# Attention with routed experts: the work behind PV two steps earlier, and the last unit of four pairs split into three and one

## The reference, cut to what matters

```python
x = x + xattn(layernorm(x), ctx_1024, ctx_1024, mask)      # softmax(q k^T / sqrt(8)) v, then Wo
...
xt = layernorm(x)
router_probs = softmax(xt @ Wr + br)
gates = max(router_probs);  idx = argmax(router_probs)
xn = layernorm(xt) * ln_g + ln_b
h = relu(xn @ W1[idx] + b1[idx])
y = (h @ W2[idx] + b2[idx]) * gates
return x + y
```

## Time and profile before

| | us |
|---|---|
| median of 3 runs (lowest to highest) | 333.48 (331.01 to 342.68) |
| the profiled execution | 330.89 |
| its span, first to last instruction | 329.2 |
| busy: PE, DVE, ACT, POOL | 253.6, 222.8, 175.0, 141.0 |

### The profile page before, as it was taken

The page is one execution under the profiler, slowest core; times in us unless marked ns, Lnnn a source line. Parts: engine busy times, 40 slices in busy tenths (PEclk is TensorE's granted clock), DMA queues, the critical chain, the costliest instruction groups (busy, mean ns, idle before and its releaser), DMA issues.

```text
span 329.2 us, 8922 instructions
## 1 busy us (share of the span) xinstructions
PE 253.6 (77%) x3112; PEld 200.9 (61%) x3112; DVE 222.8 (68%) x674; ACT 175.0 (53%) x342; POOL 141.0 (43%) x158
## 2 busy tenths in 40 slices
PE   2488999989887879888779576008897989899980
PEld 0335766767565657565667575007786878788880
DVE  6427977887788787677765545723776768677770
ACT  1528786766746584757315311006665756676640
POOL 3812343245473773634713407730443334344442
PEclk9999999999999999999965855556999999999996
DMA  8999999999999700000000001011111211212100
GB/s 233 288 252 212 279 249 206 283 271 288 257 281 291 180 19 11 27 10 2 27 8 10 28 0 34 33 42 44 41 47 45 63 50 43 60 55 65 46 28 0
DMA packets 49611, 36.31 MB, mean 110 GB/s; under 512 B 3087, under 2 KB 45460, under 8 KB 49568
## 3 DMA queue, kind: packets, MB, share of 16 engines
q1 hardware_dynamic: 46864, 31.11, 41.1%
q0 software_dynamic: 2272, 4.27, 4.0%
q10 hardware_dynamic: 432, 0.38, 0.5%
HBM read 14.11 MB, written 22.09 MB: 110 GB/s over the span
## 4 chain that ended last, share of the span: by engine, by line
issue 42%; SPq 30%; DVE 14%; DMA 6%; DVEq 3%; PE 2%; POOL 1%; POOLq 1%
SPq L240 16%; SPq L276 8%; DVE hT L701 4%; DMA out<-ot,G 4%; DVE xh L689 3%; DVE ot L710 3%; SPq L246 2%; DMA G<-rows_dram 2%; DVE yb L708 2%; DVEq L678 2%; SPq L249 2%; SPq L252 1%; PE ps L838 1%; DVE WR L681 1%; DVE VB L483 1%
## 5 line engine op out<-in xcount | busy, mean ns | idle before, releaser
L415 ACT ACTIVATE PT<-ps 128x512 f32<-128x512 f32 x64 | 35.4, 595 | 62.0 <-PE ps L757 59.6
L388 POOL DMA_INDIRECT out<-ot,G x39 | 39.8, 1020 | 65.9 <-DVE ot L710 64.9
L549 DVE TENSOR_REDUCE mx<-ps 128x16 f32<-128x1024 f32 x32 | 39.2, 1225 | 36.5 <-PE ps L733 36.4
L746 PEld LDWEIGHTS ps<-VB,PT 128*64 128x64 f32 x1024 | 35.8, 148 | 17.3 <-issue 17.3
L838 PE MATMUL ps<-xg,WR 128*128 128x128 f32 x312 | 45.3, 290 | 0.0
L746 PE MATMUL ps<-VB,PT 128*64 128x18 f32 x1024 | 38.8, 220 | 4.6 <-ACT OT L408 3.2
L849 PE MATMUL ps<-WR,hT 128*128 128x128 f32 x312 | 41.1, 275 | 0.0
L365 POOL TENSOR_TENSOR Kb<-KT,hmask 128x512 f32<-128x512 f32 x32 | 33.1, 1041 | 18.4 <-PE ps L733 18.1
L838 PEld LDWEIGHTS ps<-xg,WR 128*128 128x128 f32 x312 | 39.4, 198 | 1.4
L419 ACT ACTIVATE Pr<-Pr,rowany 128x1024 f32<-128x1024 f32 x32 | 36.7, 1148 | 5.8 <-DVE Pr L579 5.8
L579 DVE TENSOR_TENSOR Pr<-ps,mx 128x1024 f32<-128x1024 f32 x32 | 39.1, 1221 | 0.3
(11 more groups left out here) (121 smaller groups left out, 387.7 us busy)
## 6 DMA issues: line engine op xcount, KB each, us to landing
rows_dram<-empty SPq DMA_DIRECT2D x32, 528.0 KB, 9.7
WA<-in_wpk SPq DMA_DIRECT2D x8, 578.0 KB
G<-rows_dram SPq DMA_DIRECT2D x39, 66.0 KB, 1.8
X<-in_x SPq DMA_DIRECT2D x8, 256.0 KB, 7.0
C<-in_ctxT SPq DMA_DIRECT2D x8, 256.0 KB, 6.4
XT<-in_xT SPq DMA_DIRECT2D x8, 256.0 KB, 7.3
out<-ot,G POOLq DMA_INDIRECT x39, 2.3
rows_dram<-row,posi POOLq DMA_INDIRECT x32
```

The lines of the kernel that those rows point to most:

```text
L388: g.indirect_dma_start(out=out, out_offset=bass.IndirectOffsetOnAxis(ap=G[:, q, D + 1:D + 2].bitcast(I32), axis=0), in_=ot[:, q, :], in_of ...
L415: a.activation(PT[:, p % 2, 512 * m:512 * m + 512], ps[:, 4 + m, :], ACT.Copy).then_inc(freed[4 + m], 1)
L549: v.tensor_reduce(out=mx[:, i % 2, :], in_=psS.rearrange("p g (i k) -> p g i k", k=S), axis=AX.X, op=ALU.max).then_inc(s_mx, 1)
L746: last = mm(psPV[64 * b:64 * b + 64, 18 * j:18 * j + 18], PT[:, p % 2, 128 * j + 64 * b:128 * j + 64 * b + 64], VB[:, p // GP % 3, 2 * (p ...
```

## The change

Everything behind PV comes closer to it. The new stations, by lag: `onT` 2, at the end of TensorE's step instead of 3; copy to `OT` 3; `o0`, `o1` 3 and 4; `residual` 4 and 5; `ve2` 5; `pow` and `iota` 5, now at the end of GpSimd's step instead of the start; `lgm` to `lmx` 6; `lsub` to `oh` and `lex` 7; `seen` 8; `r` 9, and 8 for the last three units; `pt2` to the gate one step behind `r`; scatters 10 to 13. `xb` stays at lag 2. The last four pairs become a unit of three (28 to 30) and one of one pair (31), so there are nine units; a unit of three has all its output products in one piece. The scatters of the last three units are issued together, in one step at lag 9. Some small tiles get two buffers. The loop ends two steps earlier.

```diff
@@ -27,9 +27,10 @@
 WP = F + FC * D + FC + D
 GP = 4
 NG = NP // GP
-NU = NG
+UNITS = [(GP * g, GP) for g in range(NG - 1)] + [(NP - 4, 3), (NP - 1, 1)]
+NU = len(UNITS)
 UR = 4
-FIRST, LAST = -10, NP + 11
+FIRST, LAST = -10, NP + 9
 
 
 def wait(eng, sem, value):
@@ -40,8 +41,23 @@
 
 def unit_at(step, lag):
...
-    return u if rest == 0 and 0 <= u < NU else None
+    return next((u for u, (first, n) in enumerate(UNITS) if first + n - 1 + lag == step), None)
+
+
+def unit_of(p):
+
+    return next(u for u, (first, n) in enumerate(UNITS) if first <= p < first + n)
+
+
+def ranked_at(step):
+
+    return next((u for u, (first, n) in enumerate(UNITS) if first + n - 1 + (9 if u < NU - 3 else 8) == step), None)
+
+
+def part(u, m):
+
+    n = UNITS[u][1]
+    return range(0, min(n, 2) if n == GP else n) if m == 0 else range(2, n if n == GP else 2)
 
...
-        for name, lag in (("onT", 3), ("o0", 4), ("o1", 5), ("r", 10)):
-            if (u := unit_at(i, lag)) is not None:
+        for name, u in (("o0", unit_at(i, 3)), ("o1", unit_at(i, 4)), ("r", ranked_at(i)), ("onT", unit_at(i, 2))):
+            if u is not None and (name != "o1" or len(part(u, 1))):
                 bank[6].append((name, u))
...
-        psO = ps[:, 6, 0:2 * OW].rearrange("p (k c) -> p k c", c=OW)
+        psO = ps[:, 6, 0:3 * OW].rearrange("p (k c) -> p k c", c=OW)
...
-                if (u := unit_at(i, 7)) is not None:
-                    pool.wait_ge(s_ve2, 2 * u + 2)
-                    g.tensor_tensor(out=row[:, u % UR, :, OW + 3:RT], in0=ve2[:, u % 2, :, :],
-                                    in1=half[:, None, :].to_broadcast([P, GP, 2]), op=ALU.pow).then_inc(s_rs2, 1)
-                    g.iota(row[:, u % UR, :, OW + 1:OW + 2].bitcast(I32), pattern=[[P, GP], [0, 1]], base=GP * P * u,
-                           channel_multiplier=1).then_inc(s_tok, 1)
...
                 if (u := unit_at(i, 2)) is not None:
-                    pool.wait_ge(x_in[u], 16)
+                    first, n = UNITS[u]
+                    pool.wait_ge(x_in[first // GP], 16)
                     wait(pool, freed[6], nth("weights", 2) if u == 0 else 0)
                     if u >= 2:
-                        pool.wait_ge(freed[6], nth("o1", u - 2))
-                    g.tensor_tensor(out=xb[:, u % 2, :, E:OW], in0=X[:, GP * u:GP * u + GP, :],
-                                    in1=bo_e[:, None, E:OW].to_broadcast([P, GP, D]), op=ALU.add).then_inc(s_xb, 1)
-                for k in range(GP):
-                    if (u := unit_at(i, 11 if k == 0 or i + 1 == LAST else 11 + k)) is not None:
-                        if k == 0:
-                            pool.wait_ge(s_nm2, u + 1)
-                            pool.wait_ge(s_tok, u + 1)
-                            pool.wait_ge(s_gate, u + 1)
-                            pool.wait_ge(s_pos, u + 1)
+                        pool.wait_ge(freed[6], last_o(u - 2))
+                    g.tensor_tensor(out=xb[:, u % 2, 0:n, E:OW], in0=X[:, first:first + n, :],
+                                    in1=bo_e[:, None, E:OW].to_broadcast([P, n, D]), op=ALU.add).then_inc(s_xb, 1)
+                for u, (first, n) in enumerate(UNITS):
+                    late = u >= NU - 3
+                    at = i - (first + n - 1 + (9 if late else 10))
+                    if at == 0:
+                        pool.wait_ge(s_nm2, u + 1)
+                        pool.wait_ge(s_tok, u + 1)
+                        pool.wait_ge(s_gate, u + 1)
+                        pool.wait_ge(s_pos, u + 1)
+                    for k in range(n) if late and at == 0 else [at] if not late and 0 <= at < n else []:
                         scatter(u, k)
+                if (u := unit_at(i, 5)) is not None:
+                    first, n = UNITS[u]
+                    pool.wait_ge(s_ve2, 2 * u + 2)
+                    g.tensor_tensor(out=row[:, u % UR, 0:n, OW + 3:RT], in0=ve2[:, u % 2, 0:n, :],
+                                    in1=half[:, None, :].to_broadcast([P, n, 2]), op=ALU.pow).then_inc(s_rs2, 1)
+                    g.iota(row[:, u % UR, 0:n, OW + 1:OW + 2].bitcast(I32), pattern=[[P, n], [0, 1]], base=P * first,
+                           channel_multiplier=1).then_inc(s_tok, 1)
...
-                if (u := unit_at(i, 4)) is not None:
+                if (u := unit_at(i, 3)) is not None:
                     act.wait_ge(filled[6], nth("onT", u))
                     if u >= 1:
-                        act.wait_ge(filled[6], nth("o1", u - 1))
-                    a.activation(OT[:], ps[:, 6, :], ACT.Copy).then_inc(freed[6], 1)
+                        act.wait_ge(filled[6], last_o(u - 1))
+                    n = UNITS[u][1]
+                    a.activation(OT[:, 0:P * n], ps[:, 6, 0:P * n], ACT.Copy).then_inc(freed[6], 1)
                 if 0 <= i - 1 < NP:
...
-                if (u := unit_at(i, 9)) is not None:
+                if (u := unit_at(i, 7)) is not None:
...
+                if (u := unit_at(i, 4)) is not None:
+                    residual(u, 0)
                 if (u := unit_at(i, 5)) is not None:
-                    residual(u, 0)
-                if (u := unit_at(i, 6)) is not None:
                     residual(u, 1)
-                if (u := unit_at(i, 11)) is not None:
+                if (u := ranked_at(i - 1)) is not None:
+                    n = UNITS[u][1]
                     dve.wait_ge(filled[6], nth("r", u))
-                    v.tensor_tensor(out=pt2[:], in0=psR.rearrange("p (k e) -> p k e", e=E), in1=oh[:, u % 2, 1:GP + 1, :],
+                    v.tensor_tensor(out=pt2[:, u % 2, 0:n, :], in0=psR[:, 0:E * n].rearrange("p (k e) -> p k e", e=E), in1=oh[:, u % 2, 1:n + 1, :],
...
-                if (u := unit_at(i, 8)) is not None:
+                if (u := unit_at(i, 6)) is not None:
+                    n = UNITS[u][1]
                     dve.wait_ge(s_rs2, u + 1)
-                    v.tensor_tensor(out=lgm[:], in0=row[:, u % UR, :, 0:E], in1=row[:, u % UR, :, OW + 4:RT].to_broadcast([P, GP, E]),
+                    v.tensor_tensor(out=lgm[:, u % 2, 0:n, :], in0=row[:, u % UR, 0:n, 0:E], in1=row[:, u % UR, 0:n, OW + 4:RT].to_broadcast([P, n, E]),
                                     op=ALU.mult).then_inc(s_lgm, 1)
-                    v.scalar_tensor_tensor(out=row[:, u % UR, :, OW:OW + 1], in0=mv2[:, u % 2, :, 0:1], scalar=-1.0,
-                                           in1=row[:, u % UR, :, OW + 3:OW + 4], op0=ALU.mult, op1=ALU.mult).then_inc(s_nm2, 1)
...
-                if (u := unit_at(i, 3)) is not None:
-                    pe.wait_ge(freed[6], nth("onT", u) - 1)
-                    for k in range(GP):
-                        last = nc.tensor.transpose(ps[:, 6, P * k:P * k + P], On[:, (GP * u + k) % 8, :], ident[:])
-                    last.then_inc(filled[6], 1)
                 for m in range(2):
-                    if (u := unit_at(i, 4 + m)) is not None:
-                        pe.wait_ge(t_in[u], 16)
+                    if (u := unit_at(i, 3 + m)) is not None and len(part(u, m)):
+                        first = UNITS[u][0]
+                        pe.wait_ge(t_in[first // GP], 16)
                         pe.wait_ge(freed[6], nth(f"o{m}", u) - 1)
-                        for k in range(2):
-                            c = P * (2 * m + k)
-                            mm(psO[:, k, :], OT[:, c:c + P], Wox, start=True, stop=False, skip_group_check=True)
-                            last = mm(psO[:, k, 0:E], XT[:, GP * P * u + c:GP * P * u + c + P], Wrc[:],
+                        for k in part(u, m):
+                            o = psO[:, k - part(u, m)[0], :]
+                            mm(o, OT[:, P * k:P * k + P], Wox, start=True, stop=False, skip_group_check=True)
+                            last = mm(o[:, 0:E], XT[:, P * (first + k):P * (first + k + 1)], Wrc[:],
                                       start=False, stop=True, skip_group_check=True)
                         last.then_inc(filled[6], 1)
-                if (u := unit_at(i, 10)) is not None:
+                if (u := ranked_at(i)) is not None:
+                    n = UNITS[u][1]
                     wait(pe, s_const, 17 if u == 0 else 0)
                     pe.wait_ge(s_oh, u + 1)
                     wait(pe, s_seen, u)
                     pe.wait_ge(freed[6], nth("r", u) - 1)
-                    for k in range(GP):
-                        mm(psR[:, E * k:].rearrange("p (k e) -> p k e", e=E), ones[:],
-                           oh[:, u % 2, k:k + 1, :].to_broadcast([P, GP - k, E]), start=(k == 0), stop=False, skip_group_check=True)
-                    mm(psR, before[:], oh[:, u % 2, 1:GP + 1, :].rearrange("p k e -> p (k e)"),
+                    for k in range(n):
+                        mm(psR[:, E * k:E * n].rearrange("p (k e) -> p k e", e=E), ones[:],
+                           oh[:, u % 2, k:k + 1, :].to_broadcast([P, n - k, E]), start=(k == 0), stop=False, skip_group_check=True)
```

(43 more changed lines are left out.)

73 lines of the change are left out of this document (41 added, 32 removed).

## The result

The changed kernel takes 351.86 us (median of 4 runs, 351.24 to 354.5), the kernel before 332.25 us beside it (4 runs, 328.53 to 342.68). The ratio is 1.069 with a 95% interval of 1.057 to 1.080: slower, by 19.6 us. The prediction said 348. Every ratio here compares the fast runs of both kernels (a run over 1.5% above the fastest of its kernel is left out), while the medians are over all runs.

What follows compares the result with a forecast made beforehand. Within a loop step, what stretches VectorE ahead of `On` was taken to stretch the step, with TensorE's clock mattering too. 330.9 + 12.3 - 6.0 + 1 + 3 + 4.0 + 3 = 348 us; range 334 to 363.

Steps and rivals of the forecast that it cites:

- The block in step 1: Steps 9, 13, 17, 21, 25, 29: `Kb` and `xb` hold up VectorE's small operations, 2.05 us each, +12.3 us.
- In between: Rival: VectorE gets all it needs in between `Kb` and `xb`, no further fall of TensorE's clock; 337 us, chance 0.14.
- The sum of the loop at equal clock: Attention loop: all gains and losses without changes of TensorE's clock, +10.3 us.
- the 1 taken: Loop steps numbered 2 modulo four: `cand` meets a `Kb` in four or five steps, +1 us (bounds 0 and 2).
- The -6.0: Loop steps numbered 0 modulo four: blocking of `cand` and `lsub` by GpSimd disappears, -6.0 us.
- the neighbours: Loop: `lgm`, `nm2`, `lg`, `lmx` move into a step whose end VectorE sets, +3 us (bounds 0 and 4).
- The clock: Loop: TensorE idles about 3.4 us six times; one more fall to half clock than before, +4.0 us.
- a fall costs 4.0 us: Loop: price of one fall to half clock, from three steps taking 19.86 us against 15.82 in the same positions.
- The drain: After the loop: last `pow` waits behind five scatters; last `On` to first expert rows 28.8 us, +3 us (bounds 0 and 4).

Runs made afterwards that it cites:

- e6: Changed kernel with fourteen unread products on TensorE ahead of the transposes of `xn`, filling part of its idle time; 346.25 us, ratio 1.036 to the kernel before.
- e1: Changed kernel with `pow` and `iota` of the units of four issued one step later, behind `Kb` and `xb`; 339.29 us, ratio 1.014 to the kernel before.
- e5: Changed kernel with `xb` computed for only 8 of 128 columns; 344.89 us, ratio 1.019 to the kernel before.
- e2: Changed kernel with the scatters of unit 6 one step later, behind the last `pow`; 350.27 us, ratio 1.050 to the kernel before.
- e7: Changed kernel with the last four pairs left as one unit of four; 357.23 us, ratio 1.060 to the kernel before.

## Why the prediction was right, and where it wasn't

**The block in step 1, right.** The subtraction starts 3.65 us behind the maximum, forecast 3.55; the steps with `nm1` take 7.4 to 7.5 us at full clock (e6), forecast 7.5. e1 shows by taking `pow` away that this order is the cause. The small operations that were stretched have an excess of 5.9 (`nm2`), 2.7 (`lgm`) and 1.0 us (`nm1`), each group's busy time less its undisturbed one: 9.7 in all, against the term of 12.3. Most of the difference, 2.4 us, lies in steps 25 and 29. I kept the full 2.05 there because "there `lg` is still blocked". It wasn't: the subtraction started 2.4 us behind the maximum, between `Kb` and the end of `xb`, and the steps take 6.07 us, about 1.4 less. The lower bound of 0.9 each was right.

**"In between", wrong as a rival, right as a mechanism.** The Trainium skill (SBUF — State Buffer, "SBUF: two separate sides") holds that the port lock is kept for one instruction. In every one of these steps VectorE did get one operation in between `Kb` and `xb`, and e5 shows each operation tied to one instruction. Where a second and third operation with two SBUF operands stand behind it, the next meets `xb` and the sum is the same. So the rival fell by the reason given against it, and its mechanism is what saved the 1.4 us in steps 25 and 29. Why `cand` in the earlier trace rows waited for `Kb` and for `xb`, where `lgm` and `nm2` waited for one each, stays open. Against the rule of the same section of the Trainium skill that whoever starts first gets the shared ports stands `lsub` in e5: it started 0.20 us ahead of `Kb` and still ended with it.

**The sum of the loop at equal clock, 2.4 us too high.** Forecast +10.3, measured 7.9: e6, whose loop has one fall of the clock like that of before, is 10.4 us behind before, and 2.5 of that come from the filling (3.5 that it costs, less 1.0 by which the blocks are shorter there). Blocks in step 1 came to 9.7 instead of 12.3. In step 2 `cand` or `lsub` has 3.2 us too much over five units, less the 0.9 or so by which `lg` was stretched in two units before: 2.3 instead of the 1 taken. The -6.0 holds. What is left, 1.9 us, stands for the neighbours (+3, bounds 0 and 4); it was not measured by itself.

**The clock, right in direction, wrong in both numbers.** I took one fall more than before, at 4.0 us. Until step 31 the loop has six, in e6 one; the five more cost about 10.9 us, 2.2 each. Two steps failed. "By idle time alone all six places should have one; but one fall is all that I can see, so I take one more" set the trace's idle times aside, and they were right: all six places had one. And "a fall costs 4.0 us" came from one pair of three-step stretches, with 13.7 us at half clock; five of the falls of after last 6.8 to 10.2 us (the sixth, at 193.6, goes on into the slots). The two errors point in opposite directions, and what is left of them is 6.9 us too little. Five more falls at 4.0 us each would have given 364. The idle time itself was a slip: from 2.4 to 5.65 us behind the maximum are 3.25 us and not 3.4, and 3.26 were measured.

**The drain, right.** On to first rows: 28.0, forecast 28.8; `pow` of three pairs 6.7 us behind `On` (6.8), 1.35 long (1.35); the last scatter starts 22.3 us behind it (23.3). Against before this is +2.6, of which +2.4 shows from step 31 on; the term was +3. e2 confirms the place in the queue as its cause; by e7 the split has no part in the time from `On` on.

**The rest, and luck.** The sum of the terms as measured is 7.9 + 10.9 + 2.4 - 0.8 = 20.4, the growth of the span; forecast were 10.3 + 4.0 + 3 = 17.3. The miss of 3.1 is the clock's 6.9, less 2.4 in the loop, 0.6 in the drain and the 0.8 that the slots gave back, which I had not forecast. So the direction, the block and the drain were foreseen; that 348 came as close as it did is in part luck, because a clock term much too low met three terms that were too high.

## What to carry to other kernels

When an instruction moves in one engine's queue, write down what follows it in that queue and which small operations its reader brings with it. Here an operation of four elements took 1.27 us instead of 0.16 because a large one of GpSimd ran beside it, so the question is not what an operation costs but what runs next to it. Price an idle time of TensorE with the clock that it takes along, and look for the cheap edit that separates the two that collide (here `xb` one step later) before moving the rest.
